# Cross-attention block: score maxima over two heads at once without the mask, masked keys replaced in the loaded keys, one activation moved ahead of another

## The reference, cut to what matters

```python
x = layer_norm(hidden_states, ln1_w, ln1_b)
q, k, v = (x @ q_w + q_b), (enc @ k_w + k_b), (enc @ v_w + v_b)      # 16 heads of 32
scores = einsum('bhqd,bhkd->bhqk', q, k) / sqrt(32)
scores = where(mask, scores, finfo.min)                              # mask: 4 x 512 keys
out = einsum('bhqk,bhkd->bhqd', softmax(scores), v) @ cproj_w + cproj_b
hidden = out + residual
y = gelu(layer_norm(hidden, ln2_w, ln2_b) @ fc_w + fc_b, approximate=True) @ proj_w + proj_b
return hidden + y
```

## Time and profile before

| | us |
|---|---|
| median of 3 runs | 771.12 (771.04 to 771.34) |
| profiled execution, its own time | 771.11 |
| its span in the profile | 769.3 |
| PE busy | 744.1 (97%) |
| DVE busy | 457.1 (59%) |
| POOL busy | 299.1 (39%) |
| ACT busy | 281.4 (37%) |
| first 130 us, PE busy | 123.51 |
| 210 to 350 us (attention), PE busy | 134.15 |
| 430 us to the end (MLP), PE busy | 336.00 |

### The profile page before, as it was taken

One profiled execution on the slowest core, in us unless ns is written; L12 is line 12 of the kernel. 1 busy time (PEld: TensorE's weight loads), 2 busy tenths in 40 slices (PEclk: granted clock), 3 DMA queues, 4 the chain that ended last, 5 costly groups with the idle time before them and its releaser, 6 DMA issues.

```text
span 769.3 us, 10036 instructions
## 1 busy us (share of the span) xinstructions
PE 744.1 (97%) x3664; PEld 514.2 (67%) x3664; DVE 457.1 (59%) x995; ACT 281.4 (37%) x492; POOL 299.1 (39%) x183
## 2 busy tenths in 40 slices
PE   7999999989999999999999999999999999999998
PEld 5878886733344444444436888888888888888886
DVE  6673347778888888898697668443424333232213
ACT  4534241276766566667682011211112111211110
POOL 2654150068998778798754002212002200220000
PEclk9999999999999999999999999999999999999999
DMA  9656377597666785678641537240220413030001
GB/s 328 231 167 214 136 220 240 193 268 167 158 164 146 184 216 145 156 209 177 176 136 53 181 109 202 74 165 0 42 69 18 147 18 93 1 109 1 1 0 55
DMA packets 94385, 103.25 MB, mean 134 GB/s; under 512 B 39968, under 2 KB 48420, under 8 KB 94336
## 3 DMA queue, kind: packets, MB, share of 16 engines
q1 hardware_dynamic: 94192, 102.59, 46.5%
q10 hardware_dynamic: 144, 0.02, 0.0%
HBM read 73.08 MB, written 29.37 MB: 133 GB/s over the span
## 4 chain that ended last, share of the span: by engine, by line
PE 80%; DVE 12%; issue 3%; ACT 2%; DMA 1%; POOL 1%; SPq 0%; ACTq 0%; DVEq 0%
PE ps L487 22%; PE ps L488 21%; PE ps L489 21%; DVE ps L1009 6%; PE ps L594 4%; PE ps L610 4%; PE ps L579 4%; PE ps L625 3%; DVE R L1144 2%; ACT Pt L797 1%; PE ps L547 1%; DVE mx L1009 1%; DMA qs<-BIG 1%; DVE R L945 1%; DVE st L932 1%
## 5 line engine op out<-in xcount | busy, mean ns | idle before, releaser
L797 ACT ACTIVATE Pt<-ps 128x512 f32<-128x512 f32 x256 | 137.6, 598 | 70.9 <-PE ps L594 69.6
L1178 DVE CAST HR<-R 128x512 fp32r<-128x512 f32 x52 | 24.9, 478 | 186.0 <-ACT R L832 186.0
L832 ACT ACTIVATE R<-ps,cols 128x512 f32<-128x512 f32 x52 | 35.9, 690 | 227.2 <-PE ps L489 227.1
L594 PE MATMUL ps<-BIG 98*128 98x512 f32 x256 | 93.2, 439 | 3.6 <-ACT Pt L797 3.2
L1009 DVE CUSTOM_DVE_ANT_0 ps<-ps,FU 128x512 f32<-128x512 f32 x128 | 84.6, 724 | 14.9 <-PE ps L579 14.8
L1009 DVE CUSTOM_DVE_ANT_0 ps<-ps,BIG 128x512 f32<-128x512 f32 x128 | 84.6, 723 | 10.8 <-PE ps L579 10.7
L594 PEld LDWEIGHTS ps<-BIG 98*128 98x128 f32 x256 | 44.2, 187 | 68.3 <-issue 29.3
L487 PE MATMUL ps<-BIG,HR 128*128 128x512 f32 x192 | 74.8, 390 | 1.0 <-DVE HR L1180 1.0
L487 PE MATMUL ps<-YT,BIG 128*128 128x512 f32 x192 | 74.9, 390 | 0.0
L488 PE MATMUL ps<-YT,BIG 128*128 128x512 f32 x192 | 74.7, 389 | 0.0
L489 PE MATMUL ps<-BIG,HR 128*128 128x512 f32 x192 | 74.7, 389 | 0.0
(11 more groups left out here) (132 smaller groups left out, 1371.3 us busy)
## 6 DMA issues: line engine op xcount, KB each, us to landing
BIG<-qs SPq DMA_DIRECT2D x62, 256.0 KB, 2.8
BIG<-ks SPq DMA_DIRECT2D x62, 256.0 KB, 3.2
ks<-BIG SPq DMA_DIRECT2D x32, 256.0 KB, 2.0
qs<-BIG SPq DMA_DIRECT2D x32, 256.0 KB, 5.8
R<-hd SPq DMA_DIRECT2D x28, 256.0 KB, 3.9
R<-in_x SPq DMA_DIRECT2D x16, 256.0 KB, 5.4
hd<-R SPq DMA_DIRECT2D x16, 256.0 KB, 3.2
yt<-FU SPq DMA_DIRECT2D x64, 64.0 KB, 1.9
```

What stands on the lines that cost most here:

```text
L594: eng.matmul(bk, K_[0:98, j, kc * 128:(kc + 1) * 128], Q_[0:98, j, :], start=True, stop=True).then_inc(S["p_ra"], 1)
L797: eng.activation(Pt[:, r, j % 2, :], bank(bank_a(("s2", i, j))), ACT.Exp, scale=SCALE).then_inc(S["a_ra"], 1)
L832: eng.activation(g, bank(4 + i % 2), ACT.Gelu_apprx_tanh, bias=fcb[:, f:f + 1]).then_inc(S["a_g"], 1)
L1178: eng.tensor_copy(HR[:, n, 0, :], g).then_inc(S["v_hh"], 1)
```

## The change

Four things change. `maxima` reduces two heads (two banks, one tensor, 128x2x512) by one tensor_reduce that writes two numbers and leaves the scores as they are; 256 masked maxima become 128 plain ones. In place of the mask, the keys that are masked are replaced in the loaded leading parts before `s1` reads them, by the mean over the kept keys (`keep_sum`, `keep_part`, once for each of the 16 head groups), from two rows per batch (`kept`, `share`) that `keys` computes on DVE once for each of the 4 batches, from the mask's bytes (`load_bits`, two loads; the four `load_mask` go). The first piece's matmul of an i waits for the first pair and goes to bank 0. `copy_maxima` becomes an Identity with a bias that is nonzero only where a batch keeps no key. Last, ACT's order at the MLP's start becomes GELU 0, GELU 1, `split_out`. Two blocks of the second norm's transposes move from i = 49 and 51 to 51 and 52, since `FU` is used longer.

```diff
+        bits = [cbt[:, :].bitcast(U8), BF[:, 2048:2560].bitcast(U8)]
+        kept, share = FU[:, 0, :], FU[:, 1, :]
...
-        Y_NORM, Y_BLOCKS, Y_AFFINE = (45, 47, 49, 51), (49, 51, 53, 55), (58, 58, 58, 58)
+        Y_NORM, Y_BLOCKS, Y_AFFINE = (45, 47, 49, 51), (51, 52, 53, 55), (58, 58, 58, 58)
...
-            def load_mask(b):
-                if b >= 2:
+            def load_bits(n):
+                if n:
                     sp.wait_ge("p_pj", 40)
-                sp.wait_ge("d_mk", 16)
-                eng.dma_start(MASK[b], mk[b].partition_broadcast(128)).then_inc(S[f"d_mb{b}"], 16)
+                eng.dma_start(bits[n], mask.rearrange("b t -> (b t)").partition_broadcast(128)).then_inc(S["d_bits"], 16)
...
             def s1(group):
                 s, qc = divmod(group, 4)
                 pe.wait_ge(f"d_hi{s % 2}", 32 * (s // 2 + 1))
-                ring_b(RB[("s1", 4 * group + 3)])
+                pe.wait_ge("v_kf", s + 1)
+                place = RB[("s1", 2 * group)]
+                if place:
+                    pe.wait_ge("v_rb", place)
+                else:
+                    pe.wait_ge("v_fu", 16)
                 for j in range(4):
                     r = slice(32 * j, 32 * j + 32)
-                    eng.matmul(bank(bank_b(RB[("s1", 4 * group + j)])), lead(s)[r, 0, qc * 128:(qc + 1) * 128], lead(s)[r, 1, :],
-                               start=True, stop=True).then_inc(S["p_rb"], 1)
+                    ins = eng.matmul(bank(j), lead(s)[r, 0, qc * 128:(qc + 1) * 128], lead(s)[r, 1, :], start=True, stop=True)
+                    if j % 2:
+                        ins.then_inc(S["p_rb"], 1)
...
                     n, c, half = PIECES[i]
-                    bk = ring_b(RB[("cp", n, c, half)])
-                    cproj(n, c, (2 * half, 2 * half + 1), bk).then_inc(S["p_rb"], 1)
+                    if i in GROUPS:
+                        pe.wait_ge("v_rb", RB[("s1", 2 * GROUPS[i])] + 1)
+                    else:
+                        pe.wait_ge("v_rb", RB[("cp", n, c, half)] - 1)
+                    cproj(n, c, (2 * half, 2 * half + 1), bank(bank_cp(i))).then_inc(S["p_rb"], 1)
...
-                if i == 0:
+                if i == 1:
                     split_out(NS - 1)
...
-            def maximum(tile):
...
+            def keys(b):
+                dve.wait_ge("d_bits", 32 if b else 16)
+                eng.tensor_copy(kept, bits[1 if b else 0][:, 512 * b:512 * b + 512]).then_inc(S["v_mc"], 1)
+                dve.wait_ge("v_mc", b + 1)
+                eng.tensor_reduce(out=cnt[:, b:b + 1], in_=kept, op=ALU.add, axis=AX.X).then_inc(S["v_ct"], 1)
+                dve.wait_ge("v_ct", b + 1)
+                eng.tensor_scalar(rn[:, b:b + 1], cnt[:, b:b + 1], 1.0, -1.0, ALU.max, ALU.mult).then_inc(S["v_cm"], 1)
+                eng.tensor_scalar(nz[:, b:b + 1], cnt[:, b:b + 1], 0.0, 2.0 ** 127, ALU.is_equal, ALU.mult).then_inc(S["v_nz"], 1)
+                dve.wait_ge("v_cm", b + 1)
+                eng.reciprocal(rn[:, b:b + 1], rn[:, b:b + 1]).then_inc(S["v_rn"], 1)
+                dve.wait_ge("v_rn", b + 1)
+                eng.tensor_scalar(share, kept, 1.0, rn[:, b:b + 1], ALU.subtract, ALU.mult).then_inc(S["v_sh3"], 1)
+
+            def keep_sum(s):
+                dve.wait_ge("v_sh3", s // 4 + 1)
+                dve.wait_ge(f"d_hi{s % 2}", 32 * (s // 2 + 1))
+                part = lead(s)[:, 1, :]
+                eng.tensor_tensor_reduce(out=part, in0=part.bitcast(F32), in1=kept, scale=1.0, scalar=0.0, op0=ALU.mult,
+                                         op1=ALU.add, accum_out=ksum[:, s % 4:s % 4 + 1]).then_inc(S["v_ks"], 1)
+
+            def keep_part(s):
+                dve.wait_ge("v_ks", s + 1)
+                part = lead(s)[:, 1, :]
+                eng.scalar_tensor_tensor(out=part, in0=share, scalar=ksum[:, s % 4:s % 4 + 1], in1=part.bitcast(F32),
+                                         op0=ALU.mult, op1=ALU.add).then_inc(S["v_kf"], 1)
+
+            def maxima(n):
+                group, h = divmod(n, 2)
+                s, qc = divmod(group, 4)
+                dve.wait_ge("p_rb", RB[("s1", n)] + 1)
...
+                eng.tensor_reduce(out=mx[:, s % 2, 8 * h + qc:8 * h + qc + 5:4], in_=ps[h][:, :, :], op=ALU.max,
+                                  axis=AX.X).then_inc(S["v_rb"], 1)
...
                 if b == 3:
-                    for j in range(16):
-                        maximum(j)
+                    keep_sum(0)
+                    keep_part(0)
+                    for n in range(8):
+                        maxima(n)
+                    keep_sum(1)
+                    keep_part(1)
...
+                if b == 2:
+                    keys(0)
...
+                    if b == 3 and g == 1:
+                        keep_sum(2)
+                        keep_part(2)
...
                 if i in GROUPS:
-                    for m in range(4):
-                        maximum(4 * GROUPS[i] + m)
+                    for h in range(2):
+                        maxima(2 * GROUPS[i] + h)
+                if i in (5, 21, 37):
+                    keys((5, 21, 37).index(i) + 1)
+                if kc == 2 and s + 3 < NS:
+                    keep_sum(s + 3)
                 if kc == 2 and s >= 1:
                     divide_a(s - 1)
...
+                if kc == 2 and s + 3 < NS:
+                    keep_part(s + 3)
```

More of the change, by code:

```diff
@@ L62, in cross_attention_block @@
         mT = sb("mT", [16, 128], R)
+        kk = sb("kk", [128, 16], F32)
+        cnt, rn, nz, ksum = [kk[:, 4 * i:4 * i + 4] for i in range(4)]
         def part(base, off, k):
@@ L180, in plan_rings @@
         def plan_rings():
-            a, b, seats = {("mt", 0): 0}, {("s1", n): n for n in range(4 * EARLY)}, [("mt", 0)]
+            a, b, seats = {("mt", 0): 0}, {("s1", n): n for n in range(2 * EARLY)}, [("mt", 0)]
             for i in range(NI):
@@ L194, in plan_rings @@
                 if i in GROUPS:
-                    for j in range(4):
-                        b[("s1", 4 * GROUPS[i] + j)] = len(b)
+                    for h in range(2):
+                        b[("s1", 2 * GROUPS[i] + h)] = len(b)
                 if i in PIECES:
@@ L221, in bank_a, with bank_cp @@
             return 4 + SEAT[item] % 3
-        def bank_b(place):
-            return place % 4
+        def bank_cp(i):
+            return 2 if i in (56, 58) else 0
         def added(i, hp):
@@ L417, in _ @@
                     store_qk(*LAST_Q, 1)
+                if i == 0:
+                    load_bits(1)
                 if i == 2:
-                    load_mask(1)
-                if i in (12, 28):
-                    load_mask(2 if i == 12 else 3)
+                    sp.wait_ge("v_mc", 1)
+                    eng.dma_start(cbt[:, :], c_b.partition_broadcast(128)).then_inc(S["d_cb"], 16)
                 if i in PIECES and PIECES[i][2]:
@@ L562, in ring_a @@
                 return bank(bank_a(item))
-            def ring_b(place):
-                if place >= 4:
-                    pe.wait_ge("v_rb", place - 3)
-                else:
-                    pe.wait_ge("v_fu", 13 + place)
-                return bank(bank_b(place))
             def s1(group):
@@ L998, in qk_low @@
                     in1=QK[kq % 4][:, 0, :].bitcast(F32), op0=ALU.add, op1=ALU.subtract).then_inc(S["v_ql"], 1)
-            def maximum(tile):
-                s, n = divmod(tile, 16)
-                qc, j = divmod(n, 4)
-                place = RB[("s1", tile)]
-                dve.wait_ge("p_rb", place + 1)
+            def keys(b):
[10 more added lines that the diff above has]
+                eng.tensor_scalar(share, kept, 1.0, rn[:, b:b + 1], ALU.subtract, ALU.mult).then_inc(S["v_sh3"], 1)
@@ L1005, in maximum @@
+            def maxima(n):
+                group, h = divmod(n, 2)
+                s, qc = divmod(group, 4)
+                dve.wait_ge("p_rb", RB[("s1", n)] + 1)
                 if s >= 2:
                     dve.wait_ge("p_ra", RA[("mt", s - 2)] + 1)
-                dve.wait_ge(f"d_mb{s // 4}", 16)
-                scores = bank(bank_b(place))
-                eng.tensor_tensor_reduce(out=scores, in0=scores, in1=MASK[s // 4], scale=1.0, scalar=-3.4e38, op0=ALU.add,
-                                         op1=ALU.max, accum_out=mx[:, s % 2, 4 * j + qc:4 * j + qc + 1]).then_inc(S["v_rb"], 1)
+                eng.tensor_reduce(out=mx[:, s % 2, 8 * h + qc:8 * h + qc + 5:4], in_=ps[h][:, :, :], op=ALU.max,
+                                  axis=AX.X).then_inc(S["v_rb"], 1)
@@ L1101, in _ @@
                     if b == 3 and g in EARLY_K:
-                        for j in range(4):
-                            maximum(4 * EARLY_K[g] + j)
+                        for h in range(2):
+                            maxima(2 * EARLY_K[g] + h)
                 if b == 0:
@@ L1113, in _ @@
                     if b == 3 and g in EARLY_Q:
-                        for j in range(4):
```

(8 more changed lines are left out.)

23 lines of the change are left out of this document (10 added, 13 removed).

## The result

| | before | after |
|---|---|---|
| median | 771.08 us (4 runs) | 800.47 us (4 runs, 797.83 to 802.31) |
| ratio | | 1.0379, 95% interval 1.0345 to 1.0413 |
| profiled execution, its span | 771.11, 769.3 | 799.22, 797.4 |
| mean granted clock of TensorE | 0.999 | 0.974 |
| 210 to 350 us: PE, DVE, POOL busy | 134.15, 121.21, 116.72 | 126.20, 117.10, 101.65 |

The change costs 29.4 us where 15.3 were forecast. VectorE and POOL are *less* busy than before in the same 140 us, so neither is the bound; the engines wait for each other.

What follows compares the result with a forecast made beforehand. In the attention DVE and POOL were taken as nearly full, with PE waiting for DVE. Terms 0.3 + 4.0 + 6.1 + 6.1 - 1.2 = +15.3 us on 771.1 gave 786.4 us; range 778 to 795, with rivals 770 to 800.

Steps and rivals of the forecast that it cites:

- A set of maxima: Attention, DVE: a pair reduction takes 1.18 us, a set 2.36 instead of 2.6; each PE wait for a set shrinks 0.24.
- The swap: MLP's start: GELU 1 ahead of `split_out` removes PE's wait for DVE's second remainder, -1.2 us.
- Exclusion by POOL as the cause: DVE instructions with two SBUF inputs and POOL's SBUF-reading instructions exclude each other; the later waits. Whole forecast: chance 0.59.
- the rival in which nothing is held: POOL holds none of the new DVE instructions: +0.8 us, 772 us; chance 0.18.
- The length of a hold: A `keep` instruction waits until POOL's present instruction is over, then takes its own time; up to 2.5 us.
- s = 4 to 12: Head groups with pieces: nine delays of 0.3 to 1.85 us, together 8.0; net +6.1 us.
- the later groups would collide less: Each PE stall lets POOL catch up, so later groups collide less; left out of the sum.
- s = 0 to 3: Head groups without pieces: held `keep` instructions delay the next set and `s1`; +0.5, +1.7, +1.35, +0.4, net +4.0 us.
- The keys: `keys` at i = 21 and 37: POOL holds the scaling, delaying the piece's addition 2.8 and 3.3 us; together +6.1 us.
- The first stage: Last batch: group 1's `keep` instructions hold `s1` 1.1 us, the next `s1` loses its wait, +0.3 us; `keys(0)` costs nothing.
- POOL goes first everywhere: Rival: POOL's addition precedes the cast in three `keys`, 2.2 us more each, and pairs take 1.46 us; about 801, chance 0.10.

Runs made afterwards that it cites:

- e2: The changed kernel without `load_bits`, `keys`, `keep_sum` and `keep_part`, so maxima over two heads and the swap remain; 766.99 us, ratio 0.9936.
- e1: The kernel before with only the swapped activation (`split_out` behind the second GELU); 769.68 us, ratio 0.9981.
- e5: The changed kernel with both `keep` functions and the keys of batches 1 to 3 replaced by as many one-input reductions of about equal length; 774.13 us, ratio 1.0027.
- e16: The changed kernel with `keep_sum` written as a two-input product and a one-input reduction; 805.18 us, ratio 1.0440.
- e12: The kernel before with seven extra VectorE reductions at i = 21 and 17 useless matmuls ahead of the waiting scores at i = 22; 775.52 us, ratio 1.0060.
- e4: The changed kernel without `keys(1)` to `keys(3)`, with the replacing operations in all 16 steps; 781.95 us, ratio 1.0130.
- e7: The kernel before with seven extra VectorE reductions at i = 21, between the maxima and the piece's addition; ratio 1.0085, 6.6 us over before.
- e13: The changed kernel with 6, 11 and 20 useless matmuls ahead of the scores at i = 6, 22 and 38; 796.37 us, ratio 1.0333.
- e3: The changed kernel without `keep_sum` and `keep_part`, with all four key computations; 774.70 us, ratio 1.0053.
- e15: The changed kernel with `keep_sum` written as a scalar_tensor_tensor with accumulated output instead of the custom instruction; 792.60 us, ratio 1.0305.
- e9: The changed kernel with all keys made in the first stage, stored and reloaded per batch, and one weight-rounding activation moved; 801.60 us, ratio 1.0412.
- e7b: The kernel before with ten extra VectorE reductions at i = 21, between the maxima and the piece's addition; ratio 1.0094, 7.2 us over before.

## Why the prediction was wrong

The direction and its cause were right, the size was half. By its own steps:

- *A set of maxima.* The mean of 1218 ns is in the expected range. The pitch, which the sum uses, is 1.14 and not 1.18 us (two from 211.42, the next instruction at 213.69), so that a set gives back 0.33 instead of 0.24 us. Without the keys' part the sum's own terms come to 771.1 - 1.2 - 1.9 - 2.2 = 765.8; e2 took 766.99, and 763.5 and 764.3 in its two runs at clock 1.000.
- *The swap.* -1.2 forecast, -1.5 measured (e1).
- *Exclusion by POOL as the cause.* Right: e5 takes it away and the time falls from 800 to 774, near the 772 of the rival in which nothing is held.
- *The length of a hold: the first step that failed.* The prediction had "a `keep` instruction waits until POOL's present instruction is over". The earlier trace rows showed single additions, never a row of them. In a row a hold can last through 2 to 5 (2.45, 5.93, 6.04, 8.78 us). In the change's profile that is so at two places (5.93 and 2.45 us); the other holds end behind POOL's present instruction. e16 loses as much without a long one, so this step alone does not explain the miss. The prediction's s = 4 to 12 counted 8.0 us of delays at the places of the old trace; in the new one the collisions fall elsewhere: by the time from one step's start to the next, s = 6, 7, 10, 11 and 12 cost between -0.5 and +0.5 us, s = 4 +4.4, and s = 1, 2, 3 +3.8, +5.1, +3.8 where 1.7, 1.35 and 0.4 stood. So "the later groups would collide less", left out of the sum, was true of these. The early ones cost more: s = 0 to 3 together 13.1 us where 4.0 was forecast, nine of the missing fourteen.
- *No term for TensorE's clock: the step that failed most.* The sum priced a wait at its length and a matmul at its full speed. The profile has 41 us at half clock, and PE is busy for 19.6 us longer with the same matmuls. In s = 2 the steps from one `s1` to the next took 4.85 to 6.24 us, for the most part at half clock, without a wait for VectorE in front. Before they had taken 3.30 to 4.25, 5.1 us less in all, 0.37 per microsecond of the 13.9 at half clock. Against the same steps of s = 3 in this trace, at full clock (2.95, 2.96, 4.24), it is 5.8 us, 0.42. e12's rows give 0.44, and the runs of e4 give 0.46, where the waits may differ as well; over the whole run e12 gives 0.27. On the 41 us that makes 11 to 19 us, the greater part of the 14 that the forecast missed or more than all of it. The division between holds and clock is an estimate; that both act is shown (e5; e7 against e12, e13).
- *The keys.* 6.1 us were forecast for i = 21 and 37, and 7.7 measured for all three on e2 (e3). Beside the keeps they cost more: the steps s = 5 and 9, which hold these two, take 15.92 us each in e2's profile, 18.41 and 20.69 in e3's, and 19.88 and 22.13 in the change's. Parts that cost 7.7 and 15.0 alone cost 33.5 together, 11 more than their sum, with a clock of 0.974 in the profiled run, against 0.996 in e3's and 0.984 to 0.991 in e4.
- *The first stage.* The attention's first `s1` came 1.6 us late, 0.3 was forecast. About 0.7 of it arises between the stage's first `s1` and that one. The keeps of group 1 hold a load 1.33 us, 1.0 above the free 0.36, as forecast (1.1); but the next wait, which was to vanish, is still 0.87 where it was 1.21. The other 0.9 stood already at the stage's first `s1` (117.78 for 116.87), and its cause is open: `keys(0)` was held there (cast 2.50, scaling 1.54 us), but in e3, where it is held as long (2.51 and 1.54), this `s1` is at 116.15.

```profile
132.38 0.22 PEld L583 LDWEIGHTS ps<-YT 32*128 32x128 f32 x4 [1.33 <-issue]
139.69 0.19 PEld L583 LDWEIGHTS ps<-YT 32*128 32x128 f32 x4 [0.87 <-DVE mx L1041]
```

The rival "POOL goes first everywhere" named the right number, 801, mostly by luck. Its first half came true in part: POOL's addition was ahead of the cast at i = 5 and 37, not at i = 21. Its second half, a pair at 1.46 us, did not, and it had no term for the clock either.

## What to carry to other kernels

A VectorE operation with two inputs in SBUF is not priced by its length alone, nor always by one instruction of POOL. At worst it is held for as long as POOL's queue runs without a gap at that place, and what stands behind it waits too. The waits of 2.0 to 5.6 us that TensorE was given here cost their length and then some 0.4 us for each microsecond at half clock in which TensorE was busy. In a kernel that was at clock 1.00, price the fall as a term of its own. A change made of parts that are cheap alone should be tried with all of them together: here the whole cost 11 us more than its parts.

## What was not expected of the hardware

- A hold can outlast a row of additions by POOL (5.93 us over four, 8.78 over five), in two kinds of instruction. It is not always so: a `keep_sum` in e15 at 195.79, with 1.06 us of POOL's addition left, was let in behind it and took 1.60, and so was the custom one of the change at 161.79. What decides stays open.
- A uint8 cast is held like a scaling: 2.28 us at 319.36, and 0.43 where POOL stood still (e9, at 117.45).
- Matmuls of no use in a wait made the changed kernel faster by some 4 us (e13), just clear of the intervals.
- The Trainium skill ("TensorE: Matmul & The Clock Gate", "Terms") puts the penalty of the lower clock at half of the time spent there. The rows here come near it where TensorE is busy, 0.44 (e7 against e12) and 0.42 (s = 2). They show less where a part of the stretch lies inside a wait: in e7b 6.8 us at half clock made the step 1.7 us longer (5.96 against e12's 4.25), 0.25.
- The spread between runs grows with the falls of the clock: 1.2 us over 17 runs of the kernel before, 5.9 in e2, 8.7 in e15, the last with clocks of 0.985 to 0.974. Probably which collisions happen differs from run to run; only one run of each is traced.
